# Two conditioned attention layers on one core: early pieces, transposes and projections put in another order, GpSimd's scratch moved, fewer products and maxima ahead of the first step

## The reference

```python
# layer 0
xn = layer_norm(x, norm_w, norm_b)
q = xn @ q_w + q_b;  k = xn @ k_w + k_b;  v = (xn @ v_w + v_b) * mask      # 16 heads
att = softmax(q k^T + (1 - mask) * -1e6)                                   # 1024 x 1024 each head
y = att @ v
scale, shift = split(silu(emb) @ emb_w + emb_b)                            # the conditioning
h = layer_norm(y, sb_norm_w, sb_norm_b) * (1 + scale) + shift
x = x + silu(h) @ out_w + out_b
# layer 1: the same frame, with
q = softmax over the head's 32 channels, k = softmax over the 1024 tokens, y = q @ (k^T v)
```

## Time and profile before

| | us |
|---|---|
| median of 3 runs | 611.57 (608.18 to 619.8) |
| the profiled execution | 609.58 |
| its span | 607.4 |
| PE busy | 560.7 |
| DVE busy | 447.2 |
| ACT busy | 337.8 |
| POOL busy | 104.3 |

### The profile page before, as it was taken

The page is one execution under the profiler, slowest core; times in us unless marked ns, Lnnn a source line. Parts: engine busy times, 40 slices in busy tenths (PEclk is TensorE's granted clock), DMA queues, the critical chain, the costliest instruction groups (busy, mean ns, idle before and its releaser), DMA issues. The chain is left out here.

```text
span 607.4 us, 8411 instructions
## 1 busy us (share of the span) xinstructions
PE 560.7 (92%) x3060; PEld 274.5 (45%) x3060; DVE 447.2 (74%) x896; ACT 337.8 (56%) x411; POOL 104.3 (17%) x171
## 2 busy tenths in 40 slices
PE   8998996999999899999989999999889999987976
PEld 8554432434533343453334345455335443524765
DVE  6488674878688989887988988769888886314552
ACT  1533473555587666448667565765585566662530
POOL 4098506000000402000020230000422020002200
PEclk9999897999999999999999999999899999999998
DMA  4243985556201040404031010010002100000002
GB/s 131 80 128 74 184 273 160 140 131 143 66 27 29 2 82 0 83 1 81 25 58 28 1 28 0 6 55 19 12 2 62 35 3 2 1 0 1 1 2 69
DMA packets 18580, 33.74 MB, mean 56 GB/s; under 512 B 3930, under 2 KB 10450, under 8 KB 17772
## 3 DMA queue, kind: packets, MB, share of 16 engines
q1 hardware_dynamic: 18430, 33.18, 22.2%
q10 hardware_dynamic: 110, 0.03, 0.0%
HBM read 19.29 MB, written 13.52 MB: 54 GB/s over the span
## 5 line engine op out<-in xcount | busy, mean ns | idle before, releaser
L867 ACT ACTIVATE prob<-sT 128x1024 f32<-128x1024 f32 x256 | 247.8, 1023 | 122.0 <-PE sT L1043 121.7
L1222 DVE TENSOR_REDUCE halfmax<-bank 128x1 f32<-128x512 f32 x424 | 269.3, 684 | 60.3 <-PE bank L928 58.5
L928 PE MATMUL bank<-ks,qs 50*128 50x512 f32 x424 | 152.0, 476 | 15.2 <-DVE halfmax L1222 8.2
L1063 PE MATMUL bank<-prob,vp 128*17 128x512 f32 x1024 | 136.4, 605 | 0.6 <-ACT prob L867 0.6
L928 PEld LDWEIGHTS bank<-ks,qs 50*128 50x128 f32 x424 | 62.3, 184 | 124.9 <-DVE halfmax L1222 71.8
L1043 PE MATMUL sT<-qs,ks 52*128 52x512 f32 x512 | 105.8, 426 | 10.6 <-DMA qs<-crows 6.5
L652 POOL TENSOR_TENSOR rstd<-var,neghalf 128x4 f32<-128x4 f32 x12 | 12.2, 1015 | 430.8 <-DVE var L1146 430.8
L1043 PEld LDWEIGHTS sT<-qs,ks 52*128 52x128 f32 x512 | 53.2, 187 | 28.0 <-ACT prob L867 11.4
L1222 DVE TENSOR_REDUCE halfmax<-sT 128x1 f32<-128x512 f32 x88 | 56.8, 685 | 8.5 <-PE sT L928 7.4
L903 PE MATMUL bank<-w,hT 128*128 128x256 f32 x152 | 38.7, 388 | 1.2 <-ACT hT L789 1.2
L1063 PEld LDWEIGHTS bank<-prob,vp 128*17 128x17 f32 x1024 | 17.0, 95 | 40.4 <-issue 37.6
(11 more groups left out here) (178 smaller groups left out, 561.5 us busy)
## 6 DMA issues: line engine op xcount, KB each, us to landing
stack_rows<-late SPq DMA_DIRECT2D x12, 512.0 KB, 6.7
qs<-stack_rows SPq DMA_DIRECT2D x30, 192.0 KB, 3.4
ks<-stack_rows SPq DMA_DIRECT2D x14, 384.0 KB
stack_rows<-late SPq DMA_DIRECT2D x17, 256.0 KB, 5.0
out_x<-xs SPq DMA_DIRECT2D x4, 512.0 KB, 2.9
xs<-in_x SPq DMA_DIRECT2D x4, 256.0 KB, 3.8
xs<-in_x SPq DMA_DIRECT2D x2, 512.0 KB, 4.3
late<-in_L_cond_emb_w SPq DMA_DIRECT2D x1, 1024.0 KB, 9.2
```

The costliest lines, as they stand in the source:

```text
L867: act.activation(prob[:, c % 2, 2 * u:2 * u + 2, :].rearrange("p j n -> p (j n)"), sT[u][:, :], ACT.Exp).then_inc(exp_done, 1)
L928: last = pe.matmul(o, qs[rows, s % SLOTS, c, t * P:(t + 1) * P], ks[rows, hg, c, half * HALF:(half + 1) * HALF], start=True, stop=True)
L1063: last = pe.matmul(acc[32 * j:32 * j + VW, :], vp[:, b, c, hg * GH + j, :], prob[:, c % 2, 2 * u + two, :], start=(c == 0), stop=(c == NT ...
L1222: dve.tensor_reduce(halfmax[:, s % 2, r, half:half + 1], o, axis=AX.X, op=ALU.max, negate=True).then_inc(u.done, 1)
```

## The change

Ahead of step 0: three maxima of sub-block 1 are made ahead in place of six, the last `qk` goes before them, 8 unread products stand before the first transposes in place of 13, and 4 are added just before step 0. `halves` moves to a part of `late` that `embw` doesn't cover, and SP's wait for the second normalised half of sequence 1 ahead of the weights goes. GpSimd's centring takes a product with 1.0 and an addition in place of two additions.

In steps 0 to 21 work is put at other steps: `v` moves to step 0 and stands there ahead of the third place's maxima; the transposes of sequence 1 go to steps 1 and 3, the second half of `qk` of group 0 from step 0 to 2, the first `qk` of sequence 1 (group 4) from steps 7 and 8 to steps 4 and 5, `emb` from 4 and 5 to 7 and 8, and the rest closes up. At steps 93 to 101 the layer norm of the first half of `mid1` goes three steps ahead.

```diff
-    AHEAD = MAXES + 6
+    AHEAD = MAXES + 3
...
-        halves = late[:, TD:TD + QT * D].rearrange("p (t d) -> p t d", d=D)
+        halves = late[:, 4 * TD:4 * TD + QT * D].rearrange("p (t d) -> p t d", d=D)
...
-        put([("vec2",)], 0)
-        last = put([("qk", 0, 0, 1), ("v", 0, 3)], 0)
-        last = put([("T", "in0", 1, h, kc) for h in range(NH) for kc in range(KC)], last)
+        put([("v", 0, 3)], 0)
+        put([("T", "in0", 1, 0, kc) for kc in range(KC)], 1)
+        put([("qk", 0, 0, 1)], 2)
+        put([("vec2",)], 2)
+        last = put([("T", "in0", 1, 1, kc) for kc in range(KC)], 3)
+        last = put([("qk", 1, 0, n) for n in range(NH)], last)
         last = put([("emb", 0), ("emb", 1)], last)
-        last = put([("qk", 1, 0, n) for n in range(NH)], last)
-        last = put([("embT", 0), ("embT", 1)], last)
+        first = last + 1
         last = put([("qk", 1, hg, n) for hg in range(1, HG) for n in range(NH)], last)
         last = put([("v", 1, s) for s in range(4)], last)
+        put([("embT", 0)], first)
+        put([("embT", 1)], first + 2)
...
-        last = put([("y1", 0, s) for s in range(4)], last)
+        last = put([("y1", 0, s) for s in range(2)], last)
         layer_norm("mid1", 0, 0, last)
+        last = put([("y1", 0, s) for s in (2, 3)], last)
...
-            count = places(k) if k > 0 else [0, 0, 3, 2]
+            count = places(k) if k > 0 else [0, 2, 1, 2]
...
-        pe_beside += [pro_last[0], ("neg", 0)] + ahead[:3] + [pro_last[1]] + ahead[3:]
-        dve_beside += [("neg", 0)] + ahead[:2] + [pro_last[0]] + ahead[2:5] + [pro_last[1]] + ahead[5:]
+        pe_beside += [pro_last[0], ("neg", 0), pro_last[1]] + ahead
+        dve_beside += [("neg", 0), pro_last[0]] + ahead[:1] + [pro_last[1]] + ahead[1:]
...
-            sp.wait_ge(z_ready["in0", 1, 1], QT)
...
-                    pool.tensor_scalar(z[:, t, :], xs[:, b * NT + t, :], nmean[:, L, i:i + 1], 0.0, op0=ALU.add, op1=ALU.add).then_inc(centred, 1)
+                    pool.tensor_scalar(z[:, t, :], xs[:, b * NT + t, :], 1.0, nmean[:, L, i:i + 1], op0=ALU.mult, op1=ALU.add).then_inc(centred, 1)
...
-            unread(B8[5], 13)
+            unread(B8[5], 8)
...
+            free = unit[maxima(0, 1)[0]]
+            pe.wait_ge(free.former.done, free.former.done_at)
+            unread(free.bank, 4)
```

More of the change, by code:

```diff
@@ L296, in two_layer_conditioned_attention @@
                 dve_at[k + 2].append(("qsum", key[1], key[2] // 2))
-        act_at[1].append(("cond",))
-        dve_at[2].append(("cond",))
+        act_at[3].append(("cond",))
+        dve_at[4].append(("cond",))
         dve_at[begins["values", 0, 3] + 2].append(("recips", 0))
@@ L430, in two_layer_conditioned_attention @@
         for k in range(STEPS):
-            in_ring += maxima(k, 0) + maxima(k, 1) + maxima(k, 2) + pe_at[k]
+            in_ring += maxima(k, 0) + maxima(k, 1) + (pe_at[k] + maxima(k, 2) if k == 0 else maxima(k, 2) + pe_at[k])
         in_ring.append(("y", SUBS - 1))
@@ L1093, in _ @@
                     fill(key)
-                if k > 0:
+                if k == 0:
+                    for key in pe_at[k]:
+                        fill(key)
+                else:
                     values(k - 1)
@@ L1101, in _ @@
                     fill(key)
-                for key in pe_at[k]:
-                    fill(key)
+                if k > 0:
+                    for key in pe_at[k]:
+                        fill(key)
             values(STEPS - 1)
```

## The result

The changed kernel takes 618.70 us (median of 6 runs, 617.86 to 624.31), the kernel before 613.12 (median of 6, 608.18 to 619.8). The ratio is **1.0168 [1.0125, 1.0211]**: slower by 1.7%, in the stated range. The best estimate lies within 2%, as was forecast as likeliest, and the interval reaches a little over it. The profiled execution took 618.15 us with a span of 615.8, against 607.4 before: **+8.4 us** in the two traces.

What follows compares the result with a forecast made beforehand. Bound by PE's work and, up to 100 us, by a chain of transfers in SP's order that ends last. 609.58 + 10.4 = 620.0 for the profiled execution, 622 for the runs' median; 621 was put between them, range 611 to 629.

Steps and rivals of the forecast that it cites:

- The step that decides: Group 4's high piece, now at step 4: ACT waits for group 0's store until 98.9 us; +10.4 us at step 9.
- rival (d): ACT's stall is there, but what it holds up was not on the path; 3 to 5 us lost, 614; chance 0.08.
- rival (c): Faster, 606: group 0's store lands before ACT asks or little later; the kernels are even at 88.5; chance 0.10.
- rival (b): Prologue: clock still low in the `rep` products, 3.70 us become 7.4, transfers 3 to 4 us later; 625; chance 0.04.
- The chain of transfers: SP's transfers up to group 0's store come forward 0.9 us with the prologue and 0.7 to 0.8 from less traffic.
- The prologue: Ahead of step 0: 8 unread products in place of 13 bring the first `rep` product to 16.4 from 17.31, 0.9 us earlier.
- The clock should rise at the same instant: Ahead of step 0: PE stays at half speed up to about 14.6 us as before, so the transposes mostly run slow.
- the rule of the Trainium skill on transposes: Transposes do not count as PE activity for its clock: six products run slow, to 17.6; sum about 1 us higher.
- Steps 0 to 4: ACT's 4.74 us wait after step 0 goes; step 4 comes some 3 us earlier relative to step 0, worth nothing by itself.
- The pieces closer together: Steps 9 to 13: a slot's store must land within two steps of about 5 us; it just does, 1 us allowed.
- rival (a): More is lost, 626: stores too late for steps 11 to 16, or unmoved transfers and a later clock rise; chance 0.24.
- The rest: GpSimd's centring falls from 1146 to near 561 ns without gain; `mid1`'s earlier layer norm 0, bound 1.45 us either side.

Runs made afterwards that it cites:

- e2: Kernel before with only the pieces of group 4 moved to steps 4 and 5 and `emb` to 7 and 8: 622.13 us, ratio 1.0206.
- e3: Changed kernel with the store of group 0's second half issued right behind the store of group 3: 607.51 us, ratio 0.9938.
- e1: Changed kernel with `emb` put back at steps 4 and 5 and the pieces of group 4 at 7 and 8: 607.82 us, ratio 0.9956.
- e9: e8 plus 8 unread products in place of 13 and the layer norm of `mid1`'s first half three steps earlier: 600.69 us, ratio 0.9867.
- e6: e4 with GpSimd's part undone (old place of `halves`, centring as two additions, SP's wait back): 602.29 us, ratio 0.9862.
- e4: Changed kernel with e1's and e3's edits, and bias rows, `wo0` and layer 1's matrices issued behind `load_max(1)` and sub-block 3's queries: 602.30 us, ratio 0.9872.
- e8: Kernel before with only e4's order of transfers in SP's queue: 606.09 us, ratio 0.9898.
- e10: e4 repeated word for word, beside e9 on the same chip: 606.34 us (12 runs), ratio 0.9958.
- e5: e4 with 13 unread products ahead of the first transposes, as in the kernel before: 604.92 us, ratio 0.9879.
- e7: e4 with the layer norm of `mid1`'s first half back at its old place: 608.36 us, ratio 1.0014.

## Why the prediction was right

**The step that decides** held in its mechanism and in most numbers. Put forward from step 7 to step 4, the high piece of group 4 waited for a store that had not moved. The terms, as foretold and as measured:

| | predicted | measured |
|---|---|---|
| ACT goes on at | 98.9 | 96.07 |
| wait | some 20 us | 17.14 |
| step 5 | 6.7 | 6.40 |
| step 6 | 2.9 | 2.91 |
| steps 7 and 8 | 3.84 each | 3.84, 3.85 |
| step 9 begins | 116.9 | 113.65 |
| loss there | +10.4 | +7.15 |

The rival (d), that what is held up was off the path, is refuted by PE's 13.6 us without work and by e2. The rival (c), faster, wanted a landing before 88.5; it came at 96.07. In e3 it came at 84.76, and the ratio there was 0.994: step 9 came 4.3 us before the old 106.50, where one us for each us ahead of 88.5 gives 3.7. The rival (b) wanted slow `rep` products; they took the 3.70 us of the earlier trace rows.

**The chain of transfers** is the term that was mis-sized. I let it come forward by 0.9 us for the prologue, 0 for SP's wait, and 0.8 for less traffic beside the store. Measured: the store of group 2 came 2.24 us forward (58.48 to 56.24), the weights' issue 3.1 (69.87 to 66.76), so SP's wait of 0.9 counted there after all, the keys of group 3 2.8, and the store itself 2.7; from issue to landing it then took 6.9 us in place of 8.7. Together 4.5 us in place of 1.7, which is the whole difference between 98.9 and 96.07 and most of that between +10.4 and +7.15. That all 1.8 us of the faster landing come from less traffic is not shown: e1, where `load_max(1)` and the queries still follow the store, took 7.9 us (88.42 to 96.33), and e2, where they don't, 7.1 (91.35 to 98.43), so 0.8 to 1.8 is what the traces allow. Of the 2.8 us that this term missed, 1.3 are the prologue, 1.0 the landing, and 0.5 what the store keeps of SP's shorter wait, which I had put at 0 because the DMA engines were full.

**The prologue** gained 2.2 us by the start of group 2's store where I took 0.9. The clock rose near 7 us in this execution and near 14.6 before. In its timeline (compare):

```profile
8.09 2.05 PE L1074 MATMUL bank<-ident 128*128 128x128 f32 x16
...
11.11 1.09 PE L960 MATMUL sT<-ident,z 128*128 128x128 f32 x8 [0.97 <-DVE z L1174]
...
13.39 3.70 PE L939 MATMUL sT<-hT,late 128*128 128x512 f32 x8
```

The `rep` products came 3.9 us earlier than before. "The clock should rise at the same instant" was the reading that fell: among twelve profiled executions the rise came anywhere from about 6 to 14.6 us, with the same instructions ahead of it. Where it came as late with 8 products as before with 13, in e9 (and e6), the rows are near the ones I had worked out (12.8, 2.0, 16.4):

```profile
9.15 3.78 PE L1073 MATMUL bank<-ident 128*128 128x128 f32 x16
12.72 1.91 PE L959 MATMUL sT<-ident,z 128*128 128x128 f32 x8
14.43 1.66 PE L1073 MATMUL bank<-ident 128*128 128x128 f32 x12
15.92 2.31 PE L938 MATMUL sT<-hT,late 128*128 128x512 f32 x5
```

That is a gain of 1.4 us, the first `rep` product at 15.92 in place of 17.31. The six products behind the transposes took 1.66 us for 12 records, near the 1.50 of the high level and far from 2.7. The result that the rule of the Trainium skill on transposes ("TensorE: Matmul & The Clock Gate", PE-mode transpose) would have given here, six slow products and `rep` near 17.6, was seen in none of these executions. That does not refute the rule itself, since plain products stood on both sides of the transposes in all of them.

Of the 3.9 us `load_max(0)` and the store of group 2 kept 2.2: 1.7 were lost to a collision of DVE and GpSimd, told below. The first exponential kept only 1.4 (59.37 to 57.98). I had put the new order at 0 there; it costs 0.9 us, as the table of e4, e6, e8 and e9 shows.

**Steps 0 to 4.** The wait of 4.74 us went as predicted, worth nothing by itself. I had it as 3 us by step 4; it was 1.8 (20.8 to 19.0 us from step 0 to step 4). And "worth nothing because of what comes next" had a second reason that I didn't see: e9 against e10 shows that the order gives it back even when no store is late, 1.5 us of it in PE's wait for `scond`.

**Nothing is gained back between step 9 and the copy of step 32**: 86.02 against 85.90 us. The pieces closer together cost nothing (allowed: 1 us), and rival (a) did not come.

**The rest.** GpSimd's centring took 479 ns (561 foretold) and gained nothing, as e6 shows; that it would bring the collision was not foreseen. `mid1` had 0 with a bound of 1.45; it was 3.6 (1.9, and 1.7 at the end of the program), outside the bound, because the bound was the price of work and the gain goes with the clock. And the +5.0 us in steps 32 to 48 were not foreseen. They made the sum come out near the forecast though step 9 lost 3.2 us less: 7.15 + 5.0 - 3.6 = 8.5, against 8.4 in the spans. So the forecast's nearness to 618.70 is partly luck. The sign is not: e1 and e2 carry it.

Not tried: the copy of `cpieces` on DVE moved away from GpSimd's product, and a third slot for the pieces, which might take the wait away without touching the transfers.

## What to carry to other kernels

Before a piece of work is moved ahead, look up which transfer frees its destination and where that transfer stands in the order of the engine that issues it: here the piece went three steps forward, the store not at all, and the whole difference became a stall. A store that frees a slot belongs ahead of bulk loads that are needed later; that edit of SP's order alone gained 1% here, and the reordering of the engines' own work in steps 0 to 22 nothing on top of it. A stall that is removed ahead of a point set by a transfer, or that only lets later work pile up, is worth nothing until the sum is made at the far end.

## What the runs showed of the hardware

**Thirty nanoseconds decide over 1.7 us.** DVE's instruction with two SBUF inputs that makes the low pieces of the negative maxima takes 0.17 us. In the changed kernel GpSimd's product of 128x1024 with two inputs had begun 30 ns earlier:

```profile
51.00 1.89 POOL L716 TENSOR_TENSOR late<-z 128x1024 f32<-128x1024 f32 x1
51.03 1.88 DVE L1241 TENSOR_TENSOR cpieces<-negmax,cpieces 128x16 fp32r<-128x16 f32 x1
```

In e1, with the same prologue, DVE came 20 ns ahead of it:

```profile
51.09 0.17 DVE L1241 TENSOR_TENSOR cpieces<-negmax,cpieces 128x16 fp32r<-128x16 f32 x1
51.11 1.92 POOL L716 TENSOR_TENSOR late<-z 128x1024 f32<-128x1024 f32 x1
```

The transfer of the negatives left at 53.85 us in one and at 52.20 in the other. The Trainium skill ("GPSIMD Engine Reference", 1. Specifications) says that GpSimd shares its SBUF interfaces with VectorE and that they contend when DVE has two SBUF inputs; the two rows agree, and show the price: DVE stands until GpSimd's instruction has ended (51.03 + 1.88 = 52.91, 51.00 + 1.89 = 52.89). The same happened wherever GpSimd came first, by 30 to 60 ns (1.88 us in the changed kernel, 1.87 in e5, e7 and e10), and never where DVE did, by 20 ns (0.17 us in e1, e3 and e4).

**The granted clock differs between executions of the same order.** Steps 32 to 48 hold the same work in all twelve kernels. They took 56.1 us in four of the profiled executions (before, e1, e4, e9), 58.8 in four (e5, e6, e8, e10) and 59.6 to 61.1 in four (after, e2, e3, e7), with windows at 0.50 where it was longer. As e1 and e4 have the changed kernel's order there and show none of it, the order of those steps is not the cause. Whether the long stall before it makes such an event likelier is open. Without the 5.0 us the profiled execution of the changed kernel would have a span of 610.8, yet all six executions have 615.5 or more; without its 4.2 us e2 would have 616.2, yet its three have 618.6 or more. Two or three like it in an execution are as large as the spread of the runs of the kernel before (608 to 620 us); what sets them off stays open.
